# Edge loop of a graph attention kernel: 55 chunks in sequence in place of a register loop over pairs

## What is computed

```python
q, k, v = x @ Wq + bq, x @ Wk + bk, x @ Wv + bv     # of the normalised x; 8 heads of 32
e = edge_attr @ We
kj = k[src] + e
alpha = einsum('ehc,ehc->eh', q[dst], kj) / sqrt(32)
ea = exp(alpha - segment_max(alpha, dst)[dst])
alpha = ea / (segment_sum(ea, dst)[dst] + 1e-16)
out = segment_sum((v[src] + e) * alpha[:, :, None], dst) + (x @ Ws + bs)
x = x + out
x = x + experts(layernorm(x))                       # top 2 of 8 experts, hidden size 512
```

## Time and profile before

| what | value |
|---|---|
| median of 3 runs | 2949.69 us (2944.66 to 2949.73) |
| the profiled execution's own time | 2948.38 us |
| its span, first to last instruction | 2946.6 us |
| busy share of the span | PE 88%, PEld 74%, DVE 70%, POOL 58%, ACT 53% |
| mean granted clock of PE | 0.949 |

### The profile page before, as it was taken

The page is one execution under the profiler, slowest core; times in us unless marked ns, Lnnn a source line. Parts: engine busy times, 40 slices in busy tenths (PEclk is TensorE's granted clock), DMA queues, the critical chain, the costliest instruction groups (busy, mean ns, idle before and its releaser), DMA issues. The chain is left out here.

```text
span 2946.6 us, 81898 instructions
## 1 busy us (share of the span) xinstructions
PE 2579.8 (88%) x13731; PEld 2175.5 (74%) x13732; DVE 2050.0 (70%) x5145; ACT 1553.7 (53%) x4293; POOL 1713.2 (58%) x2023
## 2 busy tenths in 40 slices
PE   1599799999999999999999999999999447999990
PEld 0244588888888888888888888888886437999980
DVE  2655788888888888888888888888887864111116
ACT  1010266666666666666666666666666123666660
POOL 3000377777777777777777777777776312555540
PEclk9999799999999999999999999999999558999995
DMA  6123676666666666666666666666663441222217
GB/s 208 38 107 109 192 210 196 199 199 199 193 194 197 199 197 199 195 198 200 199 200 200 192 200 195 199 198 195 198 197 105 138 152 46 70 69 71 71 62 262
DMA packets 304107, 489.61 MB, mean 166 GB/s; under 512 B 52058, under 2 KB 217692, under 8 KB 303580
## 3 DMA queue, kind: packets, MB, share of 16 engines
q0 software_dynamic: 81152, 259.63, 30.4%
q1 hardware_dynamic: 215548, 214.12, 22.9%
q10 hardware_dynamic: 7056, 12.85, 1.3%
HBM read 435.86 MB, written 51.41 MB: 165 GB/s over the span
## 5 line engine op out<-in xcount | busy, mean ns | idle before, releaser
L748 POOL DMA_INDIRECT kv_ring<-vk_table,idx_c x880 | 883.0, 1003 | 743.3 <-issue 273.8
L885 PE MATMUL ps_e<-we_sb,aT 128*128 128x256 f32 x3520 | 918.0, 384 | 74.9 <-ACT aT L819 64.1
L969 DVE TENSOR_TENSOR ve_ke<-kv_ring,ps_e 128x512 f32<-128x512 f32 x880 | 602.0, 684 | 224.9 <-PE ps_e L888 128.3
L885 PEld LDWEIGHTS ps_e<-we_sb,aT 128*128 128x128 f32 x3520 | 603.6, 191 | 133.5 <-issue 35.1
L819 ACT COPY aT<-ps_t 128x256 f32<-128x256 f32 x880 | 324.8, 369 | 495.9 <-PE ps_t L873 418.9
L758 POOL TENSOR_TENSOR w_ring<-ve_ke,ea 128x264 f32<-128x264 f32 x880 | 562.0, 639 | 29.4 <-PE ps_u L938 9.1
L938 PE MATMUL ps_u<-w_ring,sel 128*128 128x264 f32 x1760 | 549.9, 395 | 7.1 <-ACT sel L801 3.3
L888 PE MATMUL ps_e<-q_sb,selT 128*128 x1760 | 528.5, 382 | 0.0
L958 DVE TENSOR_REDUCE alpha<-kqq 128x8 f32<-128x256 f32 x880 | 366.5, 417 | 35.3 <-issue 11.7
L1035 DVE TENSOR_TENSOR acc<-acc,ps_u 128x264 f32 x880 | 370.0, 420 | 29.4 <-DVE acc L1023 15.7
L888 PEld LDWEIGHTS ps_e<-q_sb,selT 128*128 128x128 f32 x1760 | 337.2, 192 | 46.6
(11 more groups left out here) (250 smaller groups left out, 2674.2 us busy)
## 6 DMA issues: line engine op xcount, KB each, us to landing
a_ring<-in_edge_attr SPq DMA_DIRECT2D x880, 128.0 KB
loc_c<-loc_table SPq DMA_DIRECT2D x55, 512.0 KB, 5.9
kv_ring<-vk_table,idx_c POOLq DMA_INDIRECT x880
vk_table<-kv_out SPq DMA_DIRECT2D x49, 256.0 KB, 2.0
got<-y_table ACTq DMA_DIRECT2D x49, 256.0 KB, 3.8
skip_table<-skip_out SPq DMA_DIRECT2D x49, 128.0 KB, 1.7
skip<-skip_table SPq DMA_DIRECT2D x7, 896.0 KB, 7.2
xn_table<-acc SPq DMA_DIRECT2D x7, 896.0 KB, 4.9
```

The source lines that it names most:

```text
L748: g.indirect_dma_start(out=kv_ring[:, i % N_KV, :], out_offset=None, in_=vk_table, in_offset=bass.IndirectOffsetOnAxis(ap=idx_c[:, par, i: ...
L885: t.matmul(ps_e[i % 2][:, 0:D], aT[i % 2][:, k * P:(k + 1) * P], we_sb[:, k, :], start=(k == 0), stop=(k == KD - 1))
L969: v.tensor_tensor(both, kv.rearrange("p (t h c) -> p t h c", t=2, c=C), by_head(e, C)[:, None, :, :].to_broadcast([P, 2, H, C]), ALU.add). ...
```

## The change

`over_chunks` no longer has a register loop. Chunks 2 to 54 are all written out, each with c as a constant, so that on all five engines the waits and offsets of these chunks are constants and there is no branch in the edge stage. The calls for chunks 0 and 1 and the two that end the lag are as before. Steps, buffers, semaphores and the order on each engine don't change.

```diff
                 emit(0, 0, plan(softmax=False, new=False, old=False, **kw))
                 emit(1, 1, plan(old=False, **kw))
-                pairs = (NCH - 2) // 2
-                with eng.Fori(0, pairs) as g:
-                    emit(g * 2 + 2, 0, plan(**kw))
-                    emit(g * 2 + 3, 1, plan(**kw))
-                for c in range(2 + 2 * pairs, NCH):
+                for c in range(2, NCH):
                     emit(c, c % 2, plan(**kw))
                 emit(NCH, NCH % 2, plan(scores=False, **kw))
```

## The result

The kernel after takes 2858.73 us (median of 4 runs, 2856.04 to 2863.48) against 2949.71 us for the kernel before beside it: a ratio of 0.9696 with a 95% interval of 0.9678 to 0.9714, or 91 us less. The profiled execution took 2858.14 us, with a span of 2856.4 us.

What follows compares the result with a forecast made beforehand. PE's matmul stream was taken to bound the edge stage. Profiled 2948.4 less 89 for the jumps, with register arithmetic, code loading and POOL's halts at zero, gave 2859.4, or 2860.7 by the median, stated as 2860; range 2849 to 2884.

Steps and rivals of the forecast that it cites:

- The jumps: Edge loop: removing 25 taken jumps back gains 87.2 to 90.9 us, taken as 89, or 3.56 a pass.
- PE's two gaps "for aT": Head of a loop pass: PE stands 1.76 and 1.80 us for aT because ACT is late after the jump.
- The second check of the 3.56: Head of a loop pass: the 3.56 us a pass is also the sum of PE's gaps, 1.76 and 1.80.
- The clock explains nothing here: Edge stage: granted clock 1.00 at the ends and 0.99 between, so it was given no share of the loss.
- What the stall is: Jump back of the edge loop: code is loaded again on q14 every pass, 301 packets in 25 passes.
- The rival that the gap belongs to a chunk's head: Chunk heads: the gap returns with constants, only branches gained, 1 to 5 us, so 2943 to 2947; chance 0.03.
- The rival of the cheap branch: Edge loop: at about 108 ns a branch, 25 jumps are worth about 3 us, result 2946; chance 0.03.
- Register arithmetic at zero: Edge loop: register work for waits and offsets lies beside PE's stream, gain zero; 11 us more if 0.22 a chunk was real.
- PE's code loading at zero: Chunks written out: q8 brings some 125 packets, 5 a pair of chunks, at no cost to PE.
- Late next: Edge stage after the change: only PE can be late; busy 67.49 us against DVE's 59.99 in the undisturbed pass.
- the rival on them: Edge stage: POOL's seven halts before gathers lose their cover, costing up to 24 us, 2884; chance 0.05.
- The mark "issue rows are gone": Waits at chunk heads: a right forecast would show the issue rows of L819, L830 and L969 gone.

Runs made afterwards that it cites:

- e12_short_shift: Against the kernel before: DVE written out, ACT's loop body cut to 321 instructions and begun 40 instructions later; 2861.53 us, ratio 0.9719.
- e3_act_dve: Against the kernel before: ACT and DVE written out, PE, SP and POOL kept in the loop of pairs; 2858.82 us, ratio 0.9708.
- e5_2x26: Against the kernel before: loop of chunks 2 to 53 made 2 passes of 26 chunks on all engines; 2869.4 us, ratio 0.9728.
- e4_others: Against the kernel before: PE, SP and POOL written out, ACT and DVE kept in the loop of pairs; 2939.28 us, ratio 0.9989.
- e9_short: Against the kernel before: DVE written out, ACT's loop body cut to 321 instructions by leaving out unwaited increments; 2910.17 us, ratio 0.9866.
- e10_pad: Against the kernel before: ACT and DVE written out, SP's loop body padded to 348 instructions and POOL's to 391; 2886.73 us, ratio 0.9794.
- e6_13x4: Against the kernel before: loop of chunks 2 to 53 made 13 passes of 4 chunks; 2961.4 us, ratio 1.0045.

## Why the prediction came out

The forecast was 2860 us with its sum of 89; the runs gave 2858.73 and the traces 89.1 for the passes. By its steps:

- **The jumps**: right in size, 87.2 to 90.9 against 89.1. Right in cause: with ACT and DVE out of the loop all of it is gained, with the others out none that its interval tells from zero. Wrong in the roles: I read PE's two gaps "for aT" as ACT's doing and took DVE as a bystander. DVE alone keeps 2.81 of the 3.56 us. The row that names a releaser tells who came last, not who would have come last but one.
- **The second check of the 3.56 agreed by luck.** The prediction found the same number as the sum of PE's two gaps at one head, 1.76 and 1.80. But the pass that holds this head took 71.43 us, 4.1 more than the undisturbed 67.34, and over the 25 passes PE's gaps come to 65.80 us, 2.6 a pass. The rest of the 3.56 is slower matmuls.
- **"The clock explains nothing here"**: wrong. The mean of 0.99 hides seven stretches of 3.4 us at 0.50, which are up to 12 of the 89 us. They follow from the gaps and went with them; the sum held because it compared whole passes with an undisturbed one.
- **What the stall is**: shown as a reload. q14 falls from 301 packets in the 25 passes to 179, and by moving ACT's code 40 instructions 125 packets and 48.6 us of the median (1.9 a pass) vanish with nothing else changed. The rival that the gap belongs to a chunk's head is out: e12_short_shift has the jumps and the heads and no gap. The rival of the cheap branch is right for a body that stays loaded (e3_act_dve: 25 jumps on three engines for 0.01 us a pass) and wrong for this one. The Trainium skill's 108 ns (Advanced Engine Details and Errata, Control Flow Timing) is the price of the branch alone; the rows have medians of 45 to 215 ns for it where the body stays loaded.
- **Register arithmetic at zero**: right. Against it stood 11 us at the lower end. e3_act_dve equals the kernel after, and e5_2x26, with registers on all engines, leaves less than 1 us outside of its jump. The 0.22 us by which chunk 54 was shorter aren't registers: written out, 46 of the chunks 2 to 53 take 33.67 us, as the undisturbed one did in the loop.
- **PE's code loading at zero**: right; e4_others has PE written out inside the old time. The count was off: 93 packets and not 125, 3.7 a pair of chunks and not 5. The first pass, from which I took the 5, ran the code of the loop, and that is longer: without the register instructions the profile has 67306 instructions where it had 81898.
- **Late next**: PE, as said; the longest chunk takes 34.90 us. POOL's halts are still there, and the rival on them is right in kind: behind the one near 1010 (2.81 us) DVE waits 1.60 us for kv_ring at 1018.62, and PE 0.99 for DVE at 1020.17. But that is nearly all of the 1.02 us that PE idles in the whole stretch, against the 24 that I left room for.
- **The mark "issue rows are gone"**: wrong as a mark. Their long pieces are gone, their sum isn't.

## What to carry to other kernels

A register loop costs nothing as long as every engine's body stays loaded, and it costs 1 to 8 us a pass once the body of an engine on or near the bound's path doesn't; look for instruction packets that come in every pass and for an engine's sequencer standing some 3 to 4 us between the branch and its next record. Go by the sequencer's own records: the idle-before column can name a semaphore's owner that was long done (e9_short), or hide the stall behind work issued earlier (POOL in e10_pad). Write out the loop for those engines, or make their body shorter; fewer passes with a longer body can be worse than the loop they replace. Before you give a gain to one engine, ask who would be late without it: two engines that stall side by side each hold back nearly all of it. And when the engine at the bound stands still, count what its work costs behind the gap too, not only the gap.

## What the runs showed of the hardware beyond that

- When the target must be loaded, the next sequencer record comes 3.4 to 4.2 us behind the branch on ACT, DVE and SP (medians of the runs) and 2.7 on POOL; on PE the branch itself lasts 5.7 (e6_13x4). When it needn't, it comes after 0.06 to 0.25 us. A second wait of ACT, with medians of 2.6 to 4.1 us, stands behind its sixth instruction where its body has the old place, and is gone where it begins 48 later.
- PE keeps a body of 1102 instructions and reloads one of 2169, with 4.8 us of idle time in the pass shown; the granted clock then is 0.50 for 3.4 to 6.8 us. ACT keeps 321 at one place and not at another.
- A packet of instructions holds 128 on q14 (8 KB) and 256 on q8 (16 KB, PE's).
- Straight code, on five engines at once for 1685 us, is loaded beside transfers at 208 GB/s with PE idle for 1.02 us in all.
